# GpSimd's program of a graph-network stack written out per tile, with indices and records read in place

## The chip, the cores and the metric

The kernel runs on one core of one Trainium2 chip. The metric is the device time of one execution in microseconds. The engines are named as in the profile: PE is TensorE (matmul; PEld its weight loads), DVE is VectorE, ACT is ScalarE, POOL is GpSimd, SP is SyncE. A "q" behind a name (POOLq) is the engine's sequencer.

## The reference

Four graph layers run one after the other on 3125 nodes with 128 features and 50,000 weighted edges. Each layer normalizes the rows, applies relu, computes a message pass over the edges, and adds the result to x:

```
x = x + L0(relu(norm(x)))   # 2 weighted sums over edges, hop 1 and hop 2, gated
x = x + L1(relu(norm(x)))   # 4-head attention, softmax over a source's edges
x = x + L2(relu(norm(x)))   # 2 transformer convolutions (4 heads, then 2)
x = x + L3(relu(norm(x)))   # degree-normalized sum over edges
# the edge step of all: out = segment_sum(weight * v[one end], other end, n)
```

So everything is one pattern: fetch a node's row for each edge, weight it, and sum by the node at the other end.

## The kernel before, in words

**The sort.** The 3125 nodes are 25 blocks of 128 (NB). Edges are sorted into tiles of 128 edges so that all edges of a tile end in one block; there are T = 416 tiles, in two orders: by source (order 0) and by destination (order 1). VectorE computes for each edge, 400 per partition (J = 400), its row in the sorted list (rowI) and its record (recE: the other end's index, the place in the block, and for order 0 the weight). POOL scatters the records to DRAM with indirect DMAs of 128 edges each, 400 per order (`scatter`); SP brings them back as `rec[o]`, 128 partitions x 416 tiles.

**The sweeps.** Nine sweeps go over all 416 tiles, in 26 rounds (G) of U = 16 tiles, and each round in two halves of HU = 8. For each tile POOL issues one indirect DMA that fetches 128 rows of a node table into `ring`, a buffer of 16 tiles (two halves), taking its 128 indices from SBUF (`gathers`). The sweeps in order: L0h1 and L0h2 (weighted sums), L1A (maxima), then L1B, which gathers nothing, L1C, L2A (maxima), L2C, L2D, L2F, and L3 (sum). VectorE builds one-hot matrices from `rec`, TensorE multiplies them with the gathered rows and so sums by block in PSUM.

**What sets the order on POOL.** One instruction list: scatter of order 0; L0h1; L0h2; the first 8 of 25 rounds of the scatter of order 1; L1A; the remaining 17 rounds, beside L1B; L1C; L2A; L2C; L2D; L2F; L3. Before each half POOL waits for its credit, a semaphore that says the half's ring slots are free: `_product` (TensorE's last matmul of the half's previous use; L0h1, L0h2, L1C, L3) or `_used` (the others; line 522). The consumers wait for `s_gath`, which the gathers raise in groups of four tiles. In the scatter POOL waits for the landing of the DMAs that last used the half's staging slots (line 494).

The scatter copies 8 indices and 8 records into `sc_idx` and `sc_rec` (496, 497), waits (498), and issues 8 DMAs (501). `sem_inc(s_gate, 1)` after each wait is an instruction of the sequencer.

## Time and profile before

| | us |
|---|---|
| median of 3 runs | 8649.6 (8616.2 to 8651.0) |
| span of the profiled execution | 8657.7 |
| POOL busy | 4762.3 (55%) |
| PE busy | 4601.0 (53%) |
| DVE busy | 3781.0 (44%) |
| ACT busy | 1975.5 (23%) |

No time of the profiled execution is given apart from its span, which is 8 us over the median of the runs. Busy time is the sum of an engine's instructions, without register, branch, semaphore and DMA-issuing ones; POOL's indirect DMAs count as busy while GpSimd works on them. A share of the whole span averages over stages whose limits differ.

### The profile page before, as it was taken

What the parts mean: (1) busy time and instruction counts of PE and PEld (TensorE: products, weight loads), DVE (VectorE), ACT (ScalarE), POOL (GpSimd) and SP (SyncE); (2) the same over time, 40 slices, a digit from 0 to 9 for tenths busy, and PEclk for the clock granted to TensorE, in tenths of its full rate; (3) what the DMA queues carried; (4) which work ended last, traced back from release to release, by engine and by line L of the source; (5) the groups of instructions that cost most, each with busy time, mean ns of one, the idle gap of its engine ahead of it and who ended that gap; (6) DMA issues with size and microseconds to landing.
All of it is one profiled execution on the core that took longest, in us unless ns stands there. A gap on an engine that the chain in (4) does not pass through costs nothing.

```text
span 8657.7 us, 87742 instructions
## 1 busy us (share of the span) xinstructions
PE 4601.0 (53%) x14994; PEld 2464.6 (28%) x14995; DVE 3781.0 (44%) x7905; ACT 1975.5 (23%) x8567; POOL 4762.3 (55%) x5225
## 2 busy tenths in 40 slices
PE   0002443332455314555677767877889986673333
PEld 0001333332111113443322222333334433442333
DVE  7501221224466525333577776663146664456111
ACT  0000000000000001101455556774024433342000
POOL 1776666677666772774344435552035645552775
PEclk9997555555566555555899988887765555555555
DMA  1000112111100002222111112221023333332112
GB/s 26 4 1 23 44 44 34 23 23 9 12 1 1 17 17 55 70 69 43 36 44 41 42 30 56 54 55 41 16 72 92 96 72 91 89 94 43 46 45 40
DMA packets 246350, 370.54 MB, mean 43 GB/s; under 512 B 111935, under 2 KB 138020, under 8 KB 246308
## 3 DMA queue, kind: packets, MB, share of 16 engines
q0 software_dynamic: 158720, 263.93, 13.5%
q1 hardware_dynamic: 87588, 106.14, 4.3%
q8 instruction: 15, 0.25, 0.0%
q14 instruction: 27, 0.22, 0.0%
HBM read 351.69 MB, written 18.07 MB: 43 GB/s over the span
## 4 chain that ended last, share of the span: by engine, by line
PE 27%; POOL 20%; issue 20%; DVE 10%; another core or an unknown queue 6%; ACT 6%; DVEq 1%; DMA 1%; POOLq 0%; ACTq 0%; SPq 0%; PEld 0%; PEldq 0%
POOL work L529 18%; PE ps L1465 7%; PE ps L1567 7%; PE ps L1449 3%; PE ps L1447 3%; ACT work L1266 2%; ACT ps L1203 2%; PE ps L1389 2%; POOL rec_by_dst L501 1%; DVE acc L803 1%; PE ps L1610 1%; DVE work L739 1%; POOL idx_slot L524 1%; DVE work L1039 1%
## 5 line engine op out<-in xcount | busy, mean ns | idle before, releaser
L529 POOL DMA_INDIRECT work<-t_h,idx_slot x1248 | 1254.4, 1005 | 482.3 <-issue 384.4
L529 POOL DMA_INDIRECT work<-t_v,idx_slot x1248 | 1238.0, 992 | 476.8 <-issue 411.9
L1567 PE MATMUL ps<-work 128*128 128x512 f32 (+1 forms) x1664 | 977.1, 708 | 308.1 <-ACT work L1266 199.4
L1345 PE MATMUL ps<-work 128*128 128x128 f32 (+1 forms) x2496 | 703.0, 453 | 819.5 <-DMA work<-t_v,idx_slot 419.1
L524 POOL COPY idx_slot<-rec_d 128x8 int32 x312 | 71.7, 230 | 1770.5 <-DVEq L838 484.2
L1465 PE MATMUL ps<-big,work 128*128 x1664 | 988.1, 689 | 84.3 <-issue 27.3
L803 DVE TENSOR_REDUCE acc<-ps 128x512 f32 (+3 forms) x1248 | 743.6, 598 | 386.5 <-PE ps L1449 236.6
L1266 ACT ACTIVATE work<-work 128x128 f32<-128x128 f32 x2496 | 795.6, 390 | 297.6 <-PE ps L1567 179.8
L1203 ACT ACTIVATE ps<-ps 128x128 f32<-128x128 f32 x2496 | 662.0, 265 | 836.6 <-DVE ps L799 630.4
L1345 PEld LDWEIGHTS ps<-work 128*128 128x128 f32 x2496 | 593.4, 328 | 892.0 <-issue 870.6
L1447 PE MATMUL ps<-work 128*128 128x512 bf16 (+1 forms) x1248 | 579.5, 464 | 318.1 <-DVE acc L803 142.4
L1033 DVE TENSOR_TENSOR acc<-acc,ps 128x512 f32 (+1 forms) x832 | 461.1, 554 | 560.8 <-PE ps L1571 307.7
L799 DVE TENSOR_TENSOR ps<-ps,work 128x512 f32<-128x512 f32 (+1 forms) x832 | 465.7, 561 | 263.1 <-PE ps L1465 128.7
L1449 PE MATMUL ps<-work 96*128 96x512 bf16 (+1 forms) x1248 | 567.5, 455 | 0.0
L654 DVE TENSOR_TENSOR work<-rec_s,iota_f 128x1024 bf16<-128x1024 f32 x104 | 127.8, 1229 | 941.9 <-remote 389.9
L529 POOL DMA_INDIRECT work<-t_xl,idx_slot x416 | 451.5, 1085 | 157.4 <-issue 121.1
L1567 PEld LDWEIGHTS ps<-work 128*128 128x128 f32 x1664 | 355.0, 264 | 630.6 <-ACT work L1266 462.8
L529 POOL DMA_INDIRECT work<-t_k,idx_slot x416 | 423.9, 1019 | 159.9 <-issue 120.3
L501 POOL DMA_INDIRECT rec_by_src<-sc_rec_s,sc_idx x400 | 407.1, 1018 | 152.9 <-issue 117.2
L529 POOL DMA_INDIRECT work<-t_sj,idx_slot x416 | 401.5, 965 | 156.9 <-issue 133.8
L501 POOL DMA_INDIRECT rec_by_dst<-sc_rec_d,sc_idx x400 | 401.3, 1003 | 154.9 <-issue 138.2
L1203 ACT ACTIVATION_READ_ACCUMULATOR ps<-ps 128x1 f32 x2496 | 474.2, 190 | 46.8 <-issue 45.5
(315 smaller groups left out, 5883.9 us busy)
## 6 DMA issues: line engine op xcount, KB each, us to landing
work<-relT_by_dst SPq DMA_DIRECT2D x260, 256.0 KB
work<-t_v,idx_slot POOLq DMA_INDIRECT x1248
work<-t_h,idx_slot POOLq DMA_INDIRECT x1248
work<-relT_by_src SPq DMA_DIRECT2D x52, 256.0 KB
work<-t_sj,idx_slot POOLq DMA_INDIRECT x416
work<-t_xl,idx_slot POOLq DMA_INDIRECT x416
work<-t_k,idx_slot POOLq DMA_INDIRECT x416
rec_by_src<-sc_rec_s,sc_idx POOLq DMA_INDIRECT x400
```

The source lines that it names most:

```text
L501: nc.gpsimd.indirect_dma_start(rec_dram[o], bass.IndirectOffsetOnAxis(ap=sc_idx[:, k:k + 1], axis=0), sc_rec[o][:, k, :], None).then_inc(s ...
L529: nc.gpsimd.indirect_dma_start(col[:, k, 0:width], None, table, bass.IndirectOffsetOnAxis(ap=idx_slot[:, k:k + 1], axis=0)).then_inc(s_gat ...
L799: V.tensor_tensor(q, q, g, ALU.mult).then_inc(sig(nq, "_multiplied"), 1)
L803: V.tensor_reduce(tile_mx[:, ds(i * U + h * HU + k, 1), 0:H].rearrange("p a h -> p (a h)"), ps[:, 4 + k % 2, 0:H * P].rearrange("p (h e) - ...
L1033: V.tensor_tensor(part, part, ps[:, k % 4, 0:H * P].unsqueeze(1), ALU.add).then_inc(sig(name, "_added"), 1)
L1203: ins = A.activation(q, q, ACT.Copy, accum_out=aS[:, h * HU + k, hd:hd + 1])
L1266: ins = A.activation(wide[:, k % 2, hd * P:(hd + 1) * P], row, ACT.Copy, scale=pA[:, h, k % HU, hd:hd + 1])
L1345: ins = M.matmul(psum_blocks[:, ds(b, 1), 0:width], oh[:, k, :], ring[:, k, 0:width].unsqueeze(1), start=False, stop=False)
L1447: M.matmul(ps[:, 4 + k % 2, 0:w].rearrange("p (h e) -> p h e", h=H), ohm[:, h * HU + k, :], low_id.unsqueeze(1).to_broadcast([P, H, P]), s ...
L1449: M.matmul(ps[:, 4 + k % 2, 0:w], pick[0:R3, k, :], spread[0:R3, h, 0:w], start=False, stop=True)\
L1465: M.matmul(ps[:, k % 4, 0:w].unsqueeze(1), ohT[:, h, k * P:(k + 1) * P], table(blocks[k]), start=True, stop=True).then_inc(sig(nq, "_q"), 1)
L1567: M.matmul(ps[:, k % 4, 0:H * P], oh[:, k, :], wide[:, k % 2, 0:H * P], start=True, stop=True)\
```

## The change

The three staging buffers (`idx_slot`, `sc_idx`, `sc_rec`) and the semaphore `s_cp` go. POOL's loops over rounds are written out: one indirect DMA instruction for each tile, 400 + 400 in the scatters and 9 x 416 in the gathers. A gather's indices are column 0 of `rec[o]` at the tile, a scatter's are a column of `rowI[o]` and its data a record of `recE[o]`. The waits for credit stand where they stood, against constants. Other engines are not touched.

```diff
--- before.py
+++ after.py
@@ -140,7 +140,6 @@
         hT = carve(1920, [CN])
         vs = carve(2560, [CB, F])
         st = sb("st", [P, 64])
-        idx_slot = sb("idx_slot", [P, U], i32)
 
         ps = ctx.enter_context(nc.psum_tensor("ps", [P, 8, 512], f32))
         psf = ps[:, :, :].rearrange("p a b -> p (a b)")
@@ -175,8 +174,6 @@
         fill = [acc[:, 4 * o:4 * o + 4, :].rearrange("p a b -> p (a b)")[:, 0:TP * RW[o]] for o in (0, 1)]
         assert o1 + 448 + 2 * T <= NB * 512
 
-        sc_idx = sb("sc_idx", [P, U], i32)
-        sc_rec = [sb("sc_rec_s", [P, U, RW[0]]), sb("sc_rec_d", [P, U, RW[1]])]
         mapI = [bigf[:, o1 + 448 + o * T:o1 + 448 + (o + 1) * T].bitcast(i32) for o in (0, 1)]
         TQ = T // 4
 
@@ -241,7 +238,6 @@
         v_s = [sem("sort_dve_s"), sem("sort_dve_d")]
         s_pref = sem("prefix")
         s_pos = sem("rows_ready")
-        s_cp = sem("scatter_slots_filled")
         s_sc = [sem("scatter_half0"), sem("scatter_half1")]
         s_scd = sem("scatter_order_done")
         s_gate = sem("pool_gate")
@@ -486,26 +482,15 @@
                     pool.wait_ge(s_filled, 32)
                     pool.sem_inc(s_gate, 1)
 
-                def body(i, first):
-                    for h in (0, 1):
-                        j = i * U + h * HU
-                        if not first:
-
-                            pool.wait_ge(s_sc[h], (i + o * SG) * HU * 16)
-                            pool.sem_inc(s_gate, 1)
-                        nc.gpsimd.tensor_copy(sc_idx[:, h * HU:(h + 1) * HU], rowI[o][:, ds(j, HU)]).then_inc(s_cp, 1)
-                        nc.gpsimd.tensor_copy(sc_rec[o][:, h * HU:(h + 1) * HU, :], recE[o][:, ds(j, HU), :]).then_inc(s_cp, 1)
-                        pool.wait_ge(s_cp, (i + o * SG) * 4 + 2 * h + 2)
+                for j in range(start * U, end * U):
+                    h, turn = (j // HU) % 2, j // U + o * SG
+                    if j % HU == 0 and turn:
+
+                        pool.wait_ge(s_sc[h], turn * HU * 16)
                         pool.sem_inc(s_gate, 1)
-                        for k in range(h * HU, (h + 1) * HU):
-                            nc.gpsimd.indirect_dma_start(
-                                rec_dram[o], bass.IndirectOffsetOnAxis(ap=sc_idx[:, k:k + 1], axis=0),
-                                sc_rec[o][:, k, :], None).then_inc(s_sc[h], 16)
-
-                if start == 0:
-                    body(0, o == 0)
-                with pool.Fori(max(start, 1), end) as i:
-                    body(i, False)
+                    nc.gpsimd.indirect_dma_start(
+                        rec_dram[o], bass.IndirectOffsetOnAxis(ap=rowI[o][:, j:j + 1], axis=0),
+                        recE[o][:, j, :], None).then_inc(s_sc[h], 16)
                 if end == SG:
                     for h in (0, 1):
                         pool.wait_ge(s_sc[h], (o + 1) * SG * HU * 16)
@@ -517,18 +502,13 @@
                 used = sig(name, "_product" if name in SUMS else "_used")
                 if name not in SUMS:
                     credit(pool, name, "_used", 2)
-                with pool.Fori(0, G) as i:
-                    for h in (0, 1):
-                        pool.wait_ge(used, nth(name, i) * 2 + h + 1)
+                for t in range(T):
+                    if t % HU == 0:
+                        pool.wait_ge(used, nth(name, 0) * 2 + t // HU + 1)
                         pool.sem_inc(s_gate, 1)
-                        nc.gpsimd.tensor_copy(idx_slot[:, h * HU:(h + 1) * HU],
-                                              rec[o][:, ds(i * U + h * HU, HU), 0].bitcast(i32)).then_inc(ph("indices"), 1)
-                        pool.wait_ge(ph("indices"), (i + rounds[name] * G) * 2 + h + 1)
-                        pool.sem_inc(s_gate, 1)
-                        for k in range(h * HU, (h + 1) * HU):
-                            nc.gpsimd.indirect_dma_start(
-                                col[:, k, 0:width], None, table,
-                                bass.IndirectOffsetOnAxis(ap=idx_slot[:, k:k + 1], axis=0)).then_inc(s_gath[k // QU], 16)
+                    nc.gpsimd.indirect_dma_start(
+                        col[:, t % U, 0:width], None, table,
+                        bass.IndirectOffsetOnAxis(ap=rec[o][:, t, 0:1].bitcast(i32), axis=0)).then_inc(s_gath[t % U // QU], 16)
 
             scatter(0, 0, SG)
             pool.wait_ge(s_rec, 16)
```

What stands on POOL in the sweep L0h1, before. The loop runs 26 times; `idx_slot` are the staged indices, `t_v` is the table, `work` holds the ring:

```order
44 L524 ISA [waits L0h1_product]
45 L524 COPY idx_slot<-rec_s 128x8
46 L529 DMA work<-t_v,idx_slot 128x128 [waits indices]
47 L529 DMA work<-t_v,idx_slot 128x128 x7
48 L522 REGISTER_ALU
49 L524 ISA [waits L0h1_product]
50 L524 COPY idx_slot<-rec_s 128x8
51 L529 DMA work<-t_v,idx_slot 128x128 [waits indices]
52 L529 DMA work<-t_v,idx_slot 128x128 x7
53 L520 REGISTER_ALU
54 L520 COMPARE_AND_BRANCH
```

The same place now, the first three halves of 52:

```order
114 L509 DMA work<-t_v,rec_s 128x128 [waits scatter_half0,scatter_half1,rec_back,n0_table,L0h1_product]
115 L509 DMA work<-t_v,rec_s 128x128 x7
116 L509 DMA work<-t_v,rec_s 128x128 [waits L0h1_product]
117 L509 DMA work<-t_v,rec_s 128x128 x7
118 L509 DMA work<-t_v,rec_s 128x128 [waits L0h1_product]
119 L509 DMA work<-t_v,rec_s 128x128 x7
```

Eight DMAs follow eight with one wait between them, that for the credit; copy, wait for the copy, and branch are gone.

POOL's loop in the scatter of order 0, before, one of its two halves (`big` holds rowI and recE):

```order
26 L496 ISA [waits scatter_half0]
27 L496 COPY sc_idx<-big 128x8
28 L497 ISA
29 L497 COPY sc_rec_s<-big 128x24
30 L498 ISA
31 L501 DMA rec_by_src<-sc_rec_s,sc_idx 54528x3 [waits scatter_slots_filled]
32 L501 DMA rec_by_src<-sc_rec_s,sc_idx 54528x3 x7
```

and now, two halves:

```order
18 L491 DMA rec_by_src<-big 54528x3 [waits scatter_half0]
19 L491 DMA rec_by_src<-big 54528x3 x7
20 L491 DMA rec_by_src<-big 54528x3 [waits scatter_half1]
21 L491 DMA rec_by_src<-big 54528x3 x7
```

Both copies and the wait for them are gone; the wait for the DMAs of the half before last stays.

## Rows read from the trace of the kernel before

**Rows 1.** The page: busy time of the engines, and POOL in 40 slices.
```profile
PE 4601.0 (53%) x14994; PEld 2464.6 (28%) x14995; DVE 3781.0 (44%) x7905; ACT 1975.5 (23%) x8567; POOL 4762.3 (55%) x5225
...
POOL 1776666677666772774344435552035645552775
```

**Rows 2.** Windows: stretch, its length, busy us (instructions) by engine, clock, DMA share, GB/s.
```profile
180.00:757.00 577.00, 20.21 (x79) 16.62 (x79) 152.00 (x275) 13.20 (x19) 424.45 (x498) 1.00 0.03 4
769.00:1404.00 635.00, 301.90 (x1263) 244.77 (x1261) 126.56 (x105) 0.00 (x0) 432.40 (x468) 0.51 0.18 43
1419.00:2027.00 608.00, 201.67 (x822) 182.97 (x822) 121.97 (x100) 0.00 (x0) 428.63 (x471) 0.50 0.14 23
...
3398.00:4036.00 638.00, 340.21 (x1661) 284.23 (x1662) 202.66 (x416) 64.01 (x104) 463.56 (x468) 0.50 0.30 68
4194.00:5150.00 956.00, 711.43 (x2101) 260.21 (x2102) 697.49 (x1377) 562.91 (x3504) 418.65 (x467) 0.93 0.17 42
...
7993.00:8609.00 616.00, 220.18 (x846) 186.88 (x844) 63.06 (x52) 0.00 (x0) 428.24 (x468) 0.50 0.19 44
```

**Rows 3.** Timeline of POOL in L0h1: start, duration, operation, [idle before, releaser].
```profile
1020.27 0.95 POOL L529 DMA_INDIRECT work<-t_v,idx_slot  x1 [0.30 <-issue]
1021.23 0.19 POOL L524 COPY idx_slot<-rec_s 128x8 int32 x1
1022.23 0.98 POOL L529 DMA_INDIRECT work<-t_v,idx_slot  x1 [0.81 <-issue]
```

**Rows 4.** Timeline of POOL in the scatter of order 0, from its first copy.
```profile
413.01 0.20 POOL L496 COPY sc_idx<-big 128x8 int32 x1
...
414.15 0.98 POOL L501 DMA_INDIRECT rec_by_src<-sc_rec_s,sc_idx  x1 [0.81 <-POOL sc_rec_s L497]
```

**Rows 5.** Waits for gathered rows (L0h2, L3, L1C): total us, times, longest.
```profile
PE ps L1345 <- DMA work<-t_v,idx_slot: 414.6, 103, 15.5
...
PE ps L1345 <- DMA work<-t_h,idx_slot: 395.8, 104, 8.2
...
DVE zE L950 <- DMA work<-t_xl,idx_slot: 138.6, 50, 10.3
```

**Rows 6.** Waits of POOL's copy in L0h1, L0h2, L3 and L1C.
```profile
POOL idx_slot L524 <- remote: 32.5, 13, 2.9
...
POOL idx_slot L524 <- remote: 19.5, 8, 3.3
...
POOL idx_slot L524 <- remote: 17.0, 7, 3.2
...
POOL idx_slot L524 <- remote: 3.7, 2, 1.9
```

**Rows 7.** Waits of POOL's copy in L2A and L1A.
```profile
POOL idx_slot L524 <- DVEq L838: 365.0, 49, 9.3
...
POOL idx_slot L524 <- DVEq L818: 53.1, 11, 7.2
```

**Rows 8.** Timelines of SP and POOL where L1A's gathers begin.
```profile
2193.29 0.37 SPq L420 DMA_DIRECT2D t_sj<-node  x1
...
2209.48 0.20 POOL L524 COPY idx_slot<-rec_s 128x8 int32 x1
```

**Rows 9.** VectorE in two windows of L1B, and its waits in the first.
```profile
2911.00:3247.00 336.00, 92.78 (x278) 0.50 0.10 22
3255.00:3388.00 133.00, 89.03 (x283) 0.50 0.16 49
...
DVE work L754 <- remote: 186.9, 20, 29.5
```

**Rows 10.** The page: the DMA queues that carry instructions.
```profile
q8 instruction: 15, 0.25, 0.0%
q14 instruction: 27, 0.22, 0.0%
```

**Rows 11.** Timeline of POOL in L3, a pause without a releaser.
```profile
8008.74 1.99 POOL L529 DMA_INDIRECT work<-t_h,idx_slot  x1 [2.04 <-issue]
```

## The prediction

> **What bounds the kernel now.** I read the page first. GpSimd (POOL) is busy 55% of the span and has work in nearly every slice from 180 us to the end, a stretch of two slices in the third quarter aside [rows 1], yet a mean says little here, because the kernel is a row of sweeps with different limits. So the second view was the table of windows, one window a stage [rows 2]. In five of them POOL is busy 68 to 74% while TensorE is busy 4 to 53% and VectorE 10 to 32%: the scatter of the source records (180 to 757), L0h1 (769 to 1404), L0h2 (1419 to 2027), L1C (3398 to 4036) and L3 (7993 to 8609). In L2A TensorE and VectorE are each busy over 70%, POOL 44%.
>
> The third view is POOL's timeline. Inside a half (8 tiles) one indirect DMA takes 0.95 us and the next starts 0.30 us after it. Between two halves stands the copy of 8 indices: 0.19 us, and then 0.81 us until the first DMA of the new half [rows 3]. From the end of one half's last DMA to the next one's first it is 1.01 us instead of 0.30. In the scatter there are two copies, and it is 1.15 us instead of 0.30 [rows 4]. A half is thus 10.7 us of which 0.7 is the copy and the wait for it.
>
> Fourth, the lists of waits say whether that 0.7 us is on the path. In L0h2 TensorE waited 103 times, 414.6 us, for gathered rows, in L3 104 times, 395.8 us; in L1C VectorE waited for them 50 times, 138.6 us [rows 5]. Those sweeps go at POOL's pace. The other way round, POOL's copy was held up by its credit (the release of a ring half) 13 times in L0h1, 8 in L0h2, 7 in L3, twice in L1C [rows 6], but 49 times in L2A, 365 us, and 11 times in L1A [rows 7]. In L2A, L2C, L2D, L2F and mostly in L1A POOL waits for the others, so a faster POOL buys nothing in the steady part.
>
> **The change part by part.** It takes away every copy on POOL and the wait behind it, 468 halves of gathers and 100 of scatters, and the loop instructions. The DMAs, their sizes, the credits and the ring with its two halves stay; the other four engines keep their programs. Per half I expect the gap to become 0.30 us, that of two DMAs in a row: saved 0.70 us in a gather and 0.85 us in a scatter. A wait with a semaphore increment stands in that gap still. What it costs behind a DMA no row shows; the nearest rows are 0.30 us (nothing between) and 0.81 us (a wait for a copy just done) [rows 3]. I take 0.30, since the copy itself starts 0.01 us after the DMA before it although the same credit wait stands ahead of it: a wait that is already satisfied is run through while the DMA is at work.
>
> The sum, against this execution's span of 8657.7 us:
> - First scatter: 49 gaps x 0.85 = 42 us. TensorE is busy 20 us and VectorE 152 of 577 there [rows 2], and the records must be back before L0h1, so all of it counts.
> - L0h1: 51 gaps less the 13 where the credit came late [rows 6], since what POOL gained in the half before is waited away there: 38 x 0.70 = 27 us. In a blocked half the way from credit to first DMA gets shorter too (no copy); bounds 0 and 1.19 + 0.81 us each. I take 3 us for all, 30.
> - L0h2: 43 x 0.70 = 30 us. L3: 44 x 0.70 = 31 us.
> - L1C: 49 x 0.70 = 34 us. Late credit is rare, so the limit behind POOL has room.
> - First third of the destination scatter, 16 halves before L1A: POOL would be done 13 us earlier, but the table that L1A's gathers read is sent only at 2193.29, some 16 us before POOL is free at 2209.48 [rows 8], and has to land. 7 us.
> - The rest of that scatter, 34 halves, runs beside L1B and is shorter by 34 x 0.85 = 29 us. L1B does not need it, yet while it runs L1B crawls: VectorE does 278 instructions in 336 us, afterwards 283 in 133 us [rows 9], and its waits there, 186.9 us in 20 times, name no releaser. If the crawl goes by time, an end 29 us earlier gives 29 x (1 - 0.83/2.13) = 18 us; if it goes by the number of scatter DMAs, about 3. I take 12.
> - Starts of L1A and of the four L2 sweeps: about 1 us each, 5 us.
> Together 42 + 30 + 30 + 31 + 34 + 7 + 12 + 5 = 191 us: a span of 8467. The median of the runs shown, 8649.6, lies 8 us under the profiled span, so 8459, 2.2% less.
>
> What is late next: in the POOL-bound sweeps still POOL, by 0.94 + 0.30 us a tile, 10.0 us a half. The ring has two halves and the consumer answers one half later, so a half that is 0.7 us shorter also leaves it 0.7 us less. The 28 late credits of L0h1, L0h2 and L3 may become more; they are blank waits ("remote"), so I can't tell their cause.
>
> **The price of a straight program.** Before, POOL runs loops of some 16 DMAs; after, each of the 4544 indirect DMAs is an instruction of its own that has to be brought in. The profile shows instruction traffic of 15 + 27 packets, 0.47 MB, for all engines together [rows 10]. Pauses of POOL with no releaser are there too, 2.04 us, with a longer DMA behind [rows 11]; they come in the loops as well, about every 110 DMAs, so they aren't the price of a straight program and stay. A DMA takes 1.25 us with its gap, so a block of instructions lasts POOL a long time, and I take 0; the bounds are 0 and a pause of 2.04 us per block, of unknown number.
>
> The Trainium skill has a rule on it (Runtime: NRT & Kernel Launch, Instruction fetch mechanics): the sequencer brings in the next 16 KiB, 256 instructions, while it executes, and only a taken branch out of its window stalls it. By that rule fetching costs nothing, and the sum above stands. Should every such block cost a pause all the same, by the page's size it would be some 10 pauses in those stages, about 20 us. No row here shows a straight POOL program, so the rule is untried by this trace.
>
> **Rivals.**
> 1. Fetching is seen, mildly: one pause of 2.04 us every 128 DMAs. The five POOL-bound stages and the destination scatter hold 2464 DMAs (400 + 4 x 416 + 400), so 19 x 2.04 = 39 us: 8498. For it: pauses of that size exist. Against: in the loops they come without any new code. Chance 0.12.
> 2. The gap isn't the copy's. The 0.81 us belongs to a wait instruction ahead of a DMA, and the credit wait inherits it. Then only the copies go, 0.20 us a gather half and 0.34 a scatter half: 49 x 0.34 + 174 x 0.20 and some us for the rest = about 60 us: 8590. For it: 0.81 follows a wait every time. Against: the copy's immediate start, above. Chance 0.07.
> 3. The late credits take it. In the sums sweeps the consumer's signal comes at its own time, POOL only waits longer, and the destination scatter's end gives nothing. First scatter aside nothing is left, and the crawl beside L1B, with denser DMAs, is 15% worse (50 us): 8650 - 42 + 50 = 8658. For it: blank waits of 3 us in three sweeps and up to 29.5 us in L1B. Against: 38 to 49 of 51 halves show no late credit. Chance 0.06.
> 4. The other way: the blank waits belong to POOL's loop and copies and go with them. L1B's 336 us at the fast rate would be 131, and the 28 blocked halves lose 69 us of waiting [rows 6]: about 250 us on top, 8210. Nothing but coincidence in time speaks for it. Chance 0.05.
> 5. Slower: POOL starves for instructions. Place: the same 2464 DMAs. Each pause costs 2.04 us, so the gain of 191 us is eaten at 94 pauses, one every 26 DMAs; at one every 16 it is 154 x 2.04 = 314 us, and the time is 8459 + 314 = 8773. For it: POOL's program held 224 indirect DMAs, which loops ran again and again, and holds 4544 now. Against: 0.47 MB of instructions in the whole span cost no visible stall of POOL. Chance 0.07.
>
> **How the numbers follow.** My forecast has 0.63, with a range of its own from 8410 to 8515: its ends are the gap at 0.45 instead of 0.30 with 3 us for L1B, and blocked halves that gain their full 2 us with 18 us for L1B. The predicted time is 8459. For eight times in ten I go from 8395 to 8595, which takes in rivals 1 and 2. A difference of 0.5%, 43 us, is about what a measurement of this kernel can tell from none: faster 0.63 + 0.12 + 0.07 + 0.05 = 0.87, within it 0.06 (rival 3), slower 0.07.
>
> **What would show it.** In the changed profile POOL has no copies, and the gap between two indirect DMAs across a half's edge reads 0.30; reading 0.8 there is rival 2. The first scatter lasts about 535 us instead of 577, L0h1 605, L0h2 578, L1C 604 and L3 585. L2A to L2F keep their lengths within 2 or 3 us each; were they shorter by 30 us, my reading of who waits there would be wrong. Instruction packets grow; pauses beyond those every 110 DMAs would be rivals 1 or 5. In L1B the number and length of the waits without a name tell between my 12 us and rivals 3 and 4.

## The result: 3.4% slower

The changed kernel takes 8915.4 us (median of 4 runs, 8908.4 to 8948.2), the kernel before beside it 8636.8 (8616.2 to 8651.0): ratio 1.034, interval 1.030 to 1.038. I had forecast 8459. The profiled execution's span is 8906.4 us, 248.7 more than before.

The page of the changed kernel, the rows that answer to [rows 1] and [rows 10]:

```profile
PE 4622.6 (52%) x14994; PEld 2467.6 (28%) x14995; DVE 3792.7 (43%) x7905; ACT 1979.3 (22%) x8567; POOL 4568.4 (51%) x4557
...
POOL 1775666775466760666144434444015554552675
...
q14 instruction: 63, 0.52, 0.0%
```

POOL has 668 instructions fewer (5225 before) and 194 us less busy time. The busy time of the others hardly moved: what was added is waiting. In POOL's slices the 10th has gone from 7 to 5, the 11th from 6 to 4 and the 16th from 2 to 0.

Windows of the changed kernel (stretch, length, busy us and instructions of PE, PEld, DVE, ACT, POOL, then clock, DMA share, GB/s), which answer to [rows 2]:

```profile
180.00:714.00 534.00, 20.21 (x79) 16.61 (x79) 121.60 (x225) 13.20 (x19) 405.84 (x400) 1.00 0.03 4
781.00:1388.00 607.00, 299.24 (x1230) 239.48 (x1228) 126.07 (x104) 0.00 (x0) 422.86 (x416) 1.00 0.18 45
...
3585.00:4206.00 621.00, 333.46 (x1630) 278.15 (x1630) 200.49 (x411) 63.78 (x103) 427.52 (x416) 0.50 0.31 70
...
8252.00:8843.00 591.00, 214.65 (x826) 182.85 (x825) 64.02 (x54) 0.00 (x0) 422.60 (x414) 0.50 0.19 46
```

The first scatter got its 42 us. But VectorE did 225 instructions in that window; before it did 275 there. The sweep L0h1 starts at 780.6, 66.2 us after POOL had finished. TensorE's granted clock in L0h1 reads 1.00 (2.4 GHz) here and 0.51 (1.2 GHz) before. It explains nothing: TensorE is busy 299 and 302 us there, and a repetition of the changed kernel (e7 below) takes the same 607 us at 0.50.

POOL's timeline in L0h1, across the edge of a half, answers to [rows 3]:

```profile
1048.70 0.94 POOL L509 DMA_INDIRECT work<-t_v,rec_s  x1 [0.30 <-issue]
1049.95 0.94 POOL L509 DMA_INDIRECT work<-t_v,rec_s  x1 [0.30 <-issue]
1051.20 0.94 POOL L509 DMA_INDIRECT work<-t_v,rec_s  x1 [0.30 <-issue]
```

Copies and rests are gone, and the median gap over an edge is 0.30 to 0.31 us in both scatters, L0h1, L0h2 and L3, as forecast. So POOL does what the change says, and the time is lost elsewhere. Stage by stage, from POOL's first indirect DMA of a stage to its last (or to the first of the next sweep, where the wait between counts):

| stage | before | after | difference | forecast |
|---|---|---|---|---|
| first scatter to start of L0h1 | 590.6 | 600.6 | +10 | -42 |
| L0h1 | 622.0 | 607.1 | -15 | -30 |
| L0h2 | 605.9 | 593.0 | -13 | -30 |
| first third of the second scatter to start of L1A | 183.5 | 292.6 | +109 | -7 |
| L1A | 646.7 | 655.1 | +8 | -1 |
| rest of the second scatter (beside L1B) to start of L1C | 540.4 | 629.4 | +89 | -12 |
| L1C | 624.0 | 621.3 | -3 | -34 |
| L2A | 945.0 | 943.7 | -1 | -1 |
| L2C | 742.8 | 819.5 | +77 | -1 |
| L2D and L2F together | 1450.9 | 1449.3 | -2 | -2 |
| L3 | 603.9 | 590.8 | -13 | -31 |

Three rows hold most of the loss, and the first row lost a gain of 42 us. In three of these four VectorE should work beside POOL's scatter; the fourth is L2C. VectorE's windows of the changed kernel, first beside the scatter, then with POOL waiting, twice over:

```profile
2007.00:2172.00 165.00, 34.57 (x95) 0.50 0.06 2
2172.00:2300.00 128.00, 54.36 (x128) 0.51 0.07 5
2956.00:3311.00 355.00, 55.69 (x145) 0.52 0.04 6
3311.00:3585.00 274.00, 164.97 (x520) 0.50 0.15 44
```

and of the kernel before, the whole first third of its second scatter:

```profile
2027.00:2210.00 183.00, 89.58 (x223) 0.50 0.14 12
```

The 223 instructions that fitted into 183 us are now 95 beside the scatter and 128 behind it. In L1B it is 145 in 355 us (2.4 us each) and then 520 in 274 (0.5 us each); in [rows 9] it was 278 in 336 us and 283 in 133. SP and POOL where L1A begins answer to [rows 8]: the table goes out at 2290.86 instead of 2193.29, and POOL has stood idle for 128.71 us.

```profile
2290.86 0.37 SPq L416 DMA_DIRECT2D t_sj<-node  x1
```
```profile
2300.35 0.97 POOL L509 DMA_INDIRECT work<-t_sj,rec_s  x1 [128.71 <-POOLq L286]
```

What VectorE does there in detail. Its timeline in the changed kernel beside the scatter:

```profile
2056.23 0.17 DVE L697 TENSOR_TENSOR st<-acc,st 128x5 f32<-128x5 f32 x1 [1.19 <-issue]
2057.64 0.17 DVE L698 TENSOR_SCALAR st<-st 128x5 f32<-128x5 f32 x1 [1.24 <-issue]
2059.03 0.17 DVE L699 TENSOR_TENSOR st<-st 128x5 f32<-128x5 f32 x1 [1.22 <-issue]
2061.13 0.19 DVE L700 RECIPROCAL st<-st 128x5 f32<-128x5 f32 x1 [1.93 <-issue]
2062.53 0.17 DVE L701 TENSOR_TENSOR st<-st 128x5 f32<-128x5 f32 x1 [1.21 <-issue]
```

Each instruction takes its usual 0.17 us, but the next one starts 1.4 to 2.1 us later, and no engine is waited for ("issue"). The page doesn't count register instructions; the trace has them, and they take more than half of that time, while nothing is recorded in the rest (start, duration, operation of VectorE's sequencer):

```
2056.88 0.71 FUSED_REGOPS
2058.28 0.70 FUSED_REGOPS
2059.69 1.39 ALU_OP
2061.77 0.70 ALU_OP
```

The median of such an instruction on VectorE is 0.04 us (ALU_OP) and 0.065 us (FUSED_REGOPS). I count the instructions of the sequencer that work on registers, branch or load a value and take over 0.5 us, and call them slow register instructions: VectorE 556 after and 47 before, TensorE 242 and 97, SP 110 and 74. On VectorE 302 lie between the start of the first scatter and L0h1, 99 between that of the second and L1A, 65 in its rest. VectorE's waits in the changed kernel's L1B answer to the wait in [rows 9]:

```profile
DVE work L734 <- remote: 145.8, 4, 41.0
```

Four waits of 36 us in the mean, and none has a releaser. In the one that ends at 3137.2 (24.8 us) TensorE runs eight matmuls of 0.17 to 0.19 us, with register instructions of 0.7 to 1.4 us between them: what VectorE waits for there is another slow sequencer. Signals are late as well. In L1C, POOL's sequencer passes the credit some 2.5 us (median) after TensorE's last matmul of the half has ended, wherever POOL is blocked. In L0h1, VectorE starts over 2 us (up to 8.7) after the matmul that it waits for in 19 of 40 waits; in the kernel before it was so in 15 of 40 (up to 8.9).

So beside a stream of indirect DMAs without rests the sequencers of other engines run slowly, and that is what the experiments look at.

### The profile page after: what moved, and what is told of

Its sections match the earlier page's. It is cut to its first block, busy times and chain, and to the rows that moved or that the text cites. A ratio compares the mean times of both kernels' runs of the same rounds, so it can differ in the third digit from the quotient of the medians.

```text
span 8906.4 us, 84294 instructions
## 1 busy us (share of the span) xinstructions
PE 4622.6 (52%) x14994; PEld 2467.6 (28%) x14995; DVE 3792.7 (43%) x7905; ACT 1979.3 (22%) x8567; POOL 4568.4 (51%) x4557
## 4 chain that ended last, share of the span: by engine, by line
PE 28%; issue 18%; POOL 18%; DVE 10%; ACT 7%; another core or an unknown queue 6%; DVEq 4%; DMA 2%; ACTq 0%; SPq 0%; POOLq 0%; PEldq 0%
POOL work L509 18%; PE ps L1547 7%; PE ps L1445 6%; PE ps L1429 4%; ACT ps L1183 3%; PE ps L1427 3%; ACT work L1246 2%; PE ps L1369 2%; DVE acc L783 1%; PE ps L1590 1%; DVEq L20 1%; DVE work L719 1%; PE ps L1325 1%; ACT work L1172 1%
## 5 line engine op out<-in xcount | busy, mean ns | idle before, releaser
L509 POOL DMA_INDIRECT work<-t_h,rec_d x1248 | 1241.4, 995 | 1482.9 <-DVEq L818 418.4
L1547 PE MATMUL ps<-work 128*128 128x512 f32 (+1 forms) x1664 | 1003.1, 727 | 325.4 <-ACT work L1246 212.6
L509 POOL DMA_INDIRECT work<-t_v,rec_s x832 | 844.6, 1015 | 448.5 <-issue 245.7
L509 POOL DMA_INDIRECT work<-t_k,rec_d x416 | 413.1, 993 | 728.6 <-DMA t_v<-big 408.3
L509 POOL DMA_INDIRECT work<-t_xl,rec_d x416 | 427.9, 1029 | 467.2 <-DMA t_xl<-node 273.8
L509 POOL DMA_INDIRECT work<-t_sj,rec_s x416 | 414.5, 996 | 369.3 <-issue 129.9
L509 POOL DMA_INDIRECT work<-t_v,rec_d x416 | 424.6, 1021 | 348.4 <-DVEq L1014 159.4
L491 POOL DMA_INDIRECT rec_by_src<-big x400 | 406.2, 1015 | 305.2 <-issue 305.2
L491 POOL DMA_INDIRECT rec_by_dst<-big x400 | 394.0, 985 | 126.1 <-issue 126.1
```

What stands on the lines that cost most here:

```text
L491: nc.gpsimd.indirect_dma_start(rec_dram[o], bass.IndirectOffsetOnAxis(ap=rowI[o][:, j:j + 1], axis=0), recE[o][:, j, :], None).then_inc(s_ ...
L509: nc.gpsimd.indirect_dma_start(col[:, t % U, 0:width], None, table, bass.IndirectOffsetOnAxis(ap=rec[o][:, t, 0:1].bitcast(i32), axis=0)). ...
L1547: M.matmul(ps[:, k % 4, 0:H * P], oh[:, k, :], wide[:, k % 2, 0:H * P], start=True, stop=True)\
```

## The experiments

**How to read them.** The kernel before read two very different times: 8637, 8813 and 8644 us in three comparisons, and 8049, 8060, 8055 and 8048 us in four others. I call the surroundings of the first three H (high) and of the other four L (low). The first experiments (L) and the next two (H) ran on the same chip some minutes apart, so it is neither the kernel nor the chip. Under L every profile has 15 slow register instructions on VectorE, 4 on TensorE and none on SP, in whichever kernel; all 19 are loads of a value, and no other one is above 0.5 us. No profile of the kernel before was taken under L; e1, which takes the same time there (1.001), stands in for it.

The traces carry a second mark. Each L trace holds 94,769 to 96,126 records of a semaphore's update, each H trace 33,854 to 47,002. For the first scatter there are 6,960 in e1 and 6,804 in e15 (both L); under H there are 6,246 in the kernel before and 853 in the changed kernel. So records are missed where the sequencers are slow. A wait without a releaser ("remote") can mean only that the record of its release is missing: VectorE has 180 such waits in the kernel before and 213 in the changed one, and no engine has one in any L trace. All times here come from recorded executions, so whether the recording itself has a part in H was not tested.

I compare only kernels that were measured together, beside the same kernel before. Theory A: POOL's rests at the edges of a half let the other sequencers work. Theory B (and B'): the written-out program does the harm, by its fetching. Theory C: the surroundings decide. Theory E: reading in place does it, whatever the rest.

**First experiments, L (before 8049.1 us).** e1: the loops written out, copies kept.

```diff
-                if start == 0:
-                    body(0, o == 0)
-                with pool.Fori(max(start, 1), end) as i:
-                    body(i, False)
+                for i in range(start, end):
+                    body(i, o == 0 and i == 0)
...
-                with pool.Fori(0, G) as i:
+                for i in range(G):
```

> The kernel before with its copies, slots and waits for them, only its POOL loops written out per round (4544 DMA instructions, as in the changed kernel). Theory A, the pause: what slows VectorE, TensorE and SyncE is that POOL no longer rests about 1 us per half; here it does, so 8600 to 8680 us, no more than 60 slow register instructions (0.7 us) of VectorE in the whole run, L1A's gathers start near 2210 us. Theory B, the straight program: its fetching or its constant waits do it, so 8850 us or more, and L1A starts near 2300.

e2: the changed kernel with a rest at each edge of a half, a memset of 8 columns and a wait for it.

```diff
+                nc.gpsimd.memset(pause[:, :], 0.0).then_inc(s_pause, 1)
+                paused[0] += 1
+                pool.wait_ge(s_pause, paused[0])
+                pool.sem_inc(s_gate, 1)
...
+                    if j % 8 == 0:
+                        rest_a_while()
...
+                    if t % 8 == 0:
+                        rest_a_while()
```

> The changed kernel (indices and records read in place, straight program) with one idle step ahead of each half: POOL zeroes 8 columns of a scratch tile and waits for that. Theory A, the pause: the gap at a half's edge is back to about 1.0 us and the time to 8600 to 8690 us, the first scatter about 570 us, L1A near 2210. Theory B, the straight program or the reading in place: still 8850 us or more, and the gap is only added on top.

e3 has only the changed kernel's `scatter` in the kernel before, e4 only its `gathers`; the other function is as it was.

> Scatters as in the changed kernel (in place, straight, no pause), gathers as before (copies, loops). Theory A, the pause: the harm sits where a scatter runs beside VectorE's own work, so most of the loss is here: the stretch from L0h2's last gather to L1A's first about 290 us instead of 185, L1A's last to L1C's first about 630 instead of 542, L1 up; 8780 to 8900 us. If the gathers did the harm, about 8600 us.

> Gathers as in the changed kernel, scatters as before (copies, loops). Theory A, the pause: 15 + 13 + 13 + 3 us come out of the sums sweeps and L1C, and L2C may lose up to 77 us as in the changed kernel: 8600 to 8700 us. If the gathers did the harm, 8850 or more.

Measured: e1 8061.3 us, 1.001 (1.000 to 1.002); e2 7950.4, 0.987 (0.986 to 0.989); e3 7972.3, 0.990 (0.989 to 0.992); e4 7882.9, 0.980 (0.978 to 0.981). Each part is a gain here and the written-out program costs nothing. That contradicts the first comparison so plainly that I ran the changed kernel again.

**Second experiments, H (before 8812.6 us).** e5 is the changed kernel, e6 the kernel before, both as they are.

> The changed kernel unchanged, once more, beside the kernel before. In the first four experiments the kernel before took 8049 us instead of 8637, and none of the 0.7 us register instructions showed. Theory C, the surroundings: where those slow instructions are absent the change does what was forecast, ratio 0.965 to 0.98 (7760 to 7890 us against 8049), with L1A's gathers starting 135 us or less after L0h2's last one. If they are present, the ratio is near 1.03 again. Theory D, both parts together: scatters and gathers in place each gained alone (0.990, 0.980), but together POOL never rests and the ratio is above 1 also where the kernel before takes 8049.

> The kernel before, unchanged, with a trace that stands beside that of the repeated changed kernel. Theory C: with 8049 us it has L1B at about 5.2 us a half also beside the scatter, and no run of 0.7 us register instructions on TensorE, VectorE or SyncE; with about 8640 us it has them as the first trace.

e5: 9048.2 us, 1.030 (1.023 to 1.036), 531 slow register instructions on VectorE. e6: 8853.8 us in one run, 157 of them, 102 in the first third of the second scatter; its L1A starts 93.9 us late where the first profile of before had 1 us. So the kernel before is slowed under H too, only less, and in that place its rests did not prevent it.

**Third experiments, H (before 8643.7 us, 19 runs).** e7 is the changed kernel, e8 is e2 again, e9 is e1, e10 is e4.

> The changed kernel as it is. Two cases, told apart by the kernel before in the same comparison. If that reads near 8050 us and its trace shows few register instructions above 0.5 us (under 20 on VectorE), both theories say that the two parts add up: 0.990 x 0.980 = 0.970, near 7810 us, with L1B hidden beside the destination scatter. If it reads near 8800 us with about 50 to 160 such instructions on VectorE, then VectorE shows over 400 of them here, the gap before L1C is 270 to 290 us, and the ratio is 1.03, as in the two comparisons of this kind so far.

> The changed kernel with one small memset of 8 columns and a wait for it at each edge of a half, so that GpSimd rests about 1 us after 8 indirect DMAs as it did before; indices are still read in place. Theory A (the rest at the edge is what lets the other engines' sequencers read their instructions in time): where the before kernel is near 8800 us, this one is not slower than it, ratio 0.985 to 1.00, VectorE's register instructions above 0.5 us are under 200 and the gap before L1C is 110 to 160 us. Theory B (it is not the rest but reading indices at an offset in the large array, or the written-out program): ratio 1.02 to 1.03 with over 400 slow register instructions, like the changed kernel. Where the before kernel is near 8050 us: 0.987 again, and it tells nothing between the theories.

> The kernel before with GpSimd's loops written out tile by tile, its index copies kept. Theory A: 1.00 within 0.01 in either condition, since the rests are still there. Theory B' (the written-out program, whose instructions have to be brought in all the time, slows the fetching of the other engines): where the before kernel is near 8800 us, ratio 1.02 to 1.03 with over 400 slow register instructions on VectorE and a gap before L1C of 250 us or more.

> Only the gathers read their indices in place; the scatters keep both copies and rests. Where the before kernel is near 8050 us: 0.980 again. Where it is near 8800 us: Theory A puts the harm beside L1B on the scatter, which is as before here: the gap before L1C is 110 to 160 us instead of 285, L0h1 to L1C are 13 us shorter each, and L2C keeps its 50 to 75 us of harm; ratio 0.995 to 1.005. Theory B' (written-out program): the gap before L1C is above 250 us all the same, ratio 1.02 or more.

| us | e7 changed | e8 rests | e9 written out | e10 gathers in place |
|---|---|---|---|---|
| ratio (interval) | 1.030 (1.025-1.036) | 1.020 (1.014-1.026) | 0.995 (0.992-0.998) | 1.011 (1.006-1.016) |
| median | 8908.6 | 8811.4 | 8612.0 | 8707.4 |
| wait of POOL before L0h1 | 66.8 | 12.7 | 12.8 | 12.5 |
| wait before L1A | 138.5 | 30.8 | 9.8 | 12.5 |
| L1A | 652.3 | 643.0 | 638.2 | 654.9 |
| scatter beside L1B + wait before L1C | 640.6 | 619.9 | 491.7 | 539.3 |
| L2C | 803.2 | 784.1 | 768.4 | 821.4 |
| VectorE, slow register instructions | 549 | 76 | 54 | 87 |
| TensorE, slow register instructions | 226 | 182 | 108 | 206 |

The rows below the median come from one profile each. That of e8 was its fastest run, 8743.1 us, 68 under its median, so its column shows less than it lost.

e9 ends theory B as a cause by itself: the program is as long as the changed one (73 instruction packets against 63) and it is the fastest of the four. Whether writing out does harm only where the rests are missing, no run under H says: none takes the rests away and keeps the loops. The Trainium skill (Runtime: NRT & Kernel Launch, Instruction fetch mechanics) says that a sequencer fetches ahead while it executes and stalls only on far branches; e1 (1.001) and e9 (0.995) agree with it.

e10 keeps the copies in the scatters and loses no time before L0h1 or L1A, so those two losses, 54 and 126 us, belong to the scatter in place. So do 101 us around L1B. The gathers in place lose in L1A (17 us), in L2C (53) and in L2D (20: 731.3 against 711.0). Around L1B, e10 (539.3) takes what the kernel before took (540.4) and e9 48 us less; the scatters of the first two are loops and that of e9 is written out.

e8 against e7 differs only in the rests. By the medians they bring back 97 of the 265 us that e7 loses against the kernel before; e8 is still 2.0% slower. The wait before L0h1 goes entirely, and the one before L1A mostly. VectorE in e7, one round of a loop beside the scatter (POOL's last DMA ends at 713.0), and two rounds after it:

```profile
607.18 0.49 DVE L598 TENSOR_SCALAR big<-big 128x400 f32<-128x400 f32 x1 [6.36 <-issue]
607.87 0.57 DVE L599 TENSOR_TENSOR big<-big 128x400 f32<-128x400 f32 x1 [0.20 <-DVE big L598]
610.67 0.65 DVE L600 SCALAR_TENSOR_TENSOR big<-big 128x416 f32<-128x416 f32 x1 [2.23 <-issue]
617.67 0.49 DVE L598 TENSOR_SCALAR big<-big 128x400 f32<-128x400 f32 x1 [6.35 <-issue]
...
740.64 0.49 DVE L598 TENSOR_SCALAR big<-big 128x400 f32<-128x400 f32 x1 [0.53 <-DVE big L600]
741.16 0.58 DVE L599 TENSOR_TENSOR big<-big 128x400 f32<-128x400 f32 x1
741.89 0.65 DVE L600 SCALAR_TENSOR_TENSOR big<-big 128x416 f32<-128x416 f32 x1 [0.15 <-DVE big L599]
743.07 0.49 DVE L598 TENSOR_SCALAR big<-big 128x400 f32<-128x400 f32 x1 [0.53 <-DVE big L600]
```

and the same loop in e8, where the scatter runs on until 748.1:

```profile
318.13 0.49 DVE L612 TENSOR_SCALAR big<-big 128x400 f32<-128x400 f32 x1 [0.36 <-DVE big L609]
318.65 0.58 DVE L613 TENSOR_TENSOR big<-big 128x400 f32<-128x400 f32 x1
319.39 0.65 DVE L614 SCALAR_TENSOR_TENSOR big<-big 128x416 f32<-128x416 f32 x1 [0.16 <-DVE big L613]
320.58 0.49 DVE L612 TENSOR_SCALAR big<-big 128x400 f32<-128x400 f32 x1 [0.54 <-DVE big L614]
```

A round takes 10.5 us beside the scatter without rests (most of the others there 11.2), 2.43 once it is over, and 2.45 beside the scatter with a rest of 0.9 us per 8 DMAs. The other profiles under H agree: mostly 11.2 us in the first one of the changed kernel and in e5, and 2.4 to 2.6 in the first one of the kernel before, e9 and e10. The work is the same and its parts of `big` don't overlap with POOL's; in e7 and e8 only the rest differs. Under H this is the cleanest pair I have, and it shows theory A beside the first scatter. Before L1A the wait fell from 138.5 to 30.8 us in this pair, yet it was 93.9 in e6 with all copies and rests, so there the rest helps and is not enough. On TensorE the rests take away little (226 to 182 slow register instructions; 108 in e9, which has rests and copies).

Around L1B it fails by half. I expected 110 to 160 us before L1C and measured 241. VectorE beside the scatter, e8 and then e10:

```profile
2850.00:3229.00 379.00, 67.29 (x181) 0.51 0.04 8
```
```profile
2850.00:3240.00 390.00, 130.71 (x373) 0.51 0.08 19
```

and e9, whose scatter is written out as that of e8 is:

```profile
2850.00:3245.00 395.00, 164.55 (x475) 0.52 0.11 25
```

The scatters have nearly the same rests, 0.91 us in e8 and 1.12 in the other two, but e8 gets 181 instructions of VectorE through, e10 373 and e9 475. Whether the missing 0.2 us decide or the reading in place itself (theory E) is not told apart by these. In its profile e8 takes 128 us more than e9 around here, which is all that it takes more in the whole span (129).

The loss in a sweep has another form. POOL in L1C of e10:

```profile
3505.39 0.94 POOL L523 DMA_INDIRECT work<-t_xl,rec_d  x1 [0.30 <-issue]
3509.22 1.43 POOL L523 DMA_INDIRECT work<-t_xl,rec_d  x1 [2.89 <-remote]
3510.96 0.94 POOL L523 DMA_INDIRECT work<-t_xl,rec_d  x1 [0.30 <-issue]
```

Every second half begins with a credit that POOL waits 2.9 us for. L1C takes 621.8 us here, and 623.0 in e9 with the 34 us of copies.

**Fourth experiments, L (before 8060.2 us).** e11 is the changed kernel with `rest_a_while()` at `j % 4 == 0` in the scatters alone. e12 is e1 with one more rest in the middle of each half beside L1B:

```diff
+                            if start and k % HU == HU // 2:
+                                rest_a_while()
```

e13 is e3 again. e14 is e1 with `gathers` in place for four sweeps:

```diff
+                if name in ("L0h1", "L0h2", "L1C", "L3"):
+                    for t in range(T):
...
+                            bass.IndirectOffsetOnAxis(ap=rec[o][:, t, 0:1].bitcast(i32), axis=0)).then_inc(s_gath[t % U // QU], 16)
+                    return
```

> The changed kernel with a rest (small memset and a wait for it, 0.6 us more between two DMAs) every 4 DMAs of both scatters; the gathers stay in place without rests. If the amount of rest sets how far VectorE, TensorE and SyncE are slowed beside the scatter (theory A), and the kernel before reads above 8600: first scatter about 600 us, no slow register instructions of VectorE in it, L1A starts under 40 us after the first third, and the destination scatter's rest plus the gap before L1C is 500 to 560 us (changed kernel 640, before 538), ratio 1.00 to 1.01, L2C still 820. If reading in place does it whatever the rest (theory E): scatter plus gap stays above 600 and the ratio above 1.02. Where the kernel before reads near 8050: scatters longer by 60 us in all, 0.985 to 0.99.

> The kernel before with loops written out, its copies kept, and one more rest in the middle of each half of the destination scatter's part beside L1B (34 rests, about 21 us longer). Theory A, where the kernel before reads above 8600: L1B gets on faster beside it, so scatter plus gap before L1C falls from 492 to 538 us to 430 to 480; ratio 0.985 to 0.99. Theory E or one in which L1B is slowed by the number of DMAs alone: scatter plus gap the same or 20 us longer, ratio 0.995 to 1.00. Where the kernel before reads near 8050, L1B is hidden and it is 20 us longer, 1.003.

> Only the scatters in place; the gathers keep copies and rests. Where the kernel before reads above 8600: the part carries the loss around L0h1 (start late by 50 us, first scatter shorter by 42), before L1A (110 to 130 us gap) and before L1C (gap 270 to 290 instead of 150), so 1.02 to 1.025, while L1A, L2C and L2D keep the lengths of before (640, 743 to 771, 710 us). If the losses before L1A and L1C come from the gathers' side instead: under 1.01. Where it reads near 8050: 0.990 again.

> Loops written out; copies kept in the scatters, L1A, L2A, L2C, L2D and L2F; indices read in place in L0h1, L0h2, L1C and L3, where GpSimd sets the pace. Where the kernel before reads above 8600: theory A says the harm of the gathers in place is in L1A, L2C and L2D, which are as before here, so what is left is 11 + 7 + 0 to 30 + 10 us of gain: ratio 0.985 to 0.995, L2C 745 to 770 us and the gap before L1C 97 to 150. If an earlier dense sweep slows the later ones: L2C above 800 all the same. Where it reads near 8050: 16 + 13 + 50 + 20 = about 100 us less, 0.988.

Measured: e11 7937.2 us, 0.985 (0.984 to 0.987); e12 8099.0, 1.005 (1.004 to 1.007); e13 7979.6, 0.990 (0.988 to 0.992); e14 7967.0, 0.989 (0.987 to 0.990). All are near what was written for L; e12 is 39 us longer where 20 were expected. Under L rests only cost time. What they do under H, which their other numbers are about, stays unmeasured.

**Fifth experiment, L (before 8055.3 us).** e15 is the changed kernel.

> The changed kernel as it is, to see it beside its own kernel before once more. Where that reads near 8050 us (few slow register instructions): theory A and C together say 0.970, near 7820 us, no gap over 15 us before L1A and L1C, fewer than 20 slow register instructions of VectorE. Where it reads 8600 to 8810: 1.03 as three times before. A theory in which the change itself brings the slow instructions in, whatever the surroundings: 1.03 in both.

7803.3 us (7783.9 to 7807.1), ratio 0.968 (0.966 to 0.970). The very kernel that loses 3% three times under H gains 3.2% here. Its POOL streams just as densely: median gap 0.30 us over the edges of the scatter beside VectorE's work and of L1B. The same lines of VectorE as above, in e15:

```profile
1952.90 0.17 DVE L697 TENSOR_TENSOR st<-acc,st 128x5 f32<-128x5 f32 x1
1953.10 0.17 DVE L698 TENSOR_SCALAR st<-st 128x5 f32<-128x5 f32 x1
1953.30 0.17 DVE L699 TENSOR_TENSOR st<-st 128x5 f32<-128x5 f32 x1
1953.50 0.19 DVE L700 RECIPROCAL st<-st 128x5 f32<-128x5 f32 x1
```

Four starts within 0.6 us instead of 4.9, beside the same stream. e15 has 15 slow register instructions on VectorE. Its windows for VectorE, beside the first third of the second scatter and beside the rest of it:

```profile
1881.00:2051.00 170.00, 89.61 (x223) 0.51 0.08 2
2609.00:2969.00 360.00, 223.62 (x663) 0.51 0.16 37
```

All 223 instructions and nearly all of L1B fit beside the scatters, and POOL waits 3.9 us before L1A and 10.7 before L1C. In L0h1, VectorE starts 0.17 us after the matmul that it waits for, all 50 times. Theory C holds: the stream without rests does no harm by itself; it does where the surroundings are H.

**Sixth experiments, L (before 8048.2 us).** e16, e17 and e18 are e12, e13 and e14 once more.

> Written-out loops, copies kept, one more rest in the middle of each half of the scatter part beside L1B. Where the kernel before reads above 8600, theory A (rests set how far L1B is slowed): scatter plus gap before L1C 430 to 480 us instead of 492 to 538, ratio 0.985 to 0.99. If the slowing goes by the number of DMAs: 510 to 540, ratio 0.995 to 1.00. Near 8055: 1.005 as measured.

> Only the scatters in place. Where the kernel before reads above 8600: L0h1 starts as late as before although the scatter ends 42 us earlier, gap before L1A 110 to 130 us, before L1C 270 to 290, L1A, L2C, L2D as before; 1.02 to 1.025. If the gathers' side causes the gaps: under 1.01. Near 8055: 0.990 as measured twice.

> In place only in L0h1, L0h2, L1C and L3. Where the kernel before reads above 8600: 0.985 to 0.995, L2C 745 to 770 us and the gap before L1C 97 to 150 us, if the harm of the gathers lies in L1A, L2C and L2D; L2C above 800 if an earlier dense sweep does it. Near 8055: 0.989 as measured.

Measured: e16 8098.8 us, 1.006 (1.004 to 1.008); e17 7974.9, 0.991 (0.989 to 0.993); e18 7973.2, 0.991 (0.989 to 0.992). They repeat e12, e13 and e14 within 0.2% and decide nothing about H.

No version beats both kernels in both surroundings. Under L it is the changed kernel itself, 0.968. Under H it is e9 by 0.5%, which is as small as the difference that I had called measurable. e14 keeps the copies wherever a loss was seen under H; that it would be the safe choice is an inference, since it ran only under L.

## Why the prediction was wrong

**The step that failed** is "the other four engines keep their programs", with the work that was to hide each edit. I asked of each rest only whether it lies on POOL's own path, and costed it for the others at nothing, or at a gain (L1B, 12 us). Under H VectorE's sequencer keeps its pace beside the first scatter only where POOL rests (e7 against e8), and work that was hidden comes to lie on the path. The rests are not all of it: with them back and the reading still in place (e8), 168 of the 265 us lost are lost still. Between my sum (-191) and the two spans (+249) lie 440 us. By the table 52 of them came before L0h1, 116 before L1A, 101 before L1C and 78 in L2C, together 347; of the other 93, 81 are gains that came too small in L0h1, L0h2, L1C and L3, 9 are L1A, and 3 lie outside the table.

**First scatter, -42.** Right for POOL (-42), wrong for the path. I wrote that VectorE is busy 152 of 577 us, so all of it counts. A quarter busy is true at VectorE's usual pace. With 1.4 us from one short instruction to the next, its work outlasts the scatter. e7 against e8 shows it.

**L0h1, L0h2, L3, -30 each.** 13 to 15 came under H, 13 to 24 under L (e1 to e15, which were not measured together: 572.9 to 556.4, 576.0 to 563.4, 579.1 to 555.6; e4, measured with e1, gives 16, 13 and 20). The edge gap is 0.30, as I took it, so rival 2 is refuted. But the DMAs themselves became longer: 1.033 us in the mean in L0h1 of e15, 0.972 in e1, which over 416 is 25 of the 36 us that 52 edges save. The term was right in kind and too large by half.

**L1C, -34.** -3 under H and -48 under L. Under H the late credit [rows 6] takes it, which I had judged rare because it stood at 2 of 51: with 0.7 us less slack it came 24 times in the changed kernel (68.2 us) and in e10 (67.8 us). Under L it came in none, and the DMAs there were shorter too (1.060 us against 1.092), which is 13 us of the 48. The prediction had named this as what could be late next, and gave it no price.

**First third of the second scatter, -7.** I read from [rows 8] that POOL was free 16 us after the table was sent, and took the table's time as fixed. It was set by VectorE beside the same scatter, and moved by 97.6 us. Under H it was not even fixed in the kernel before (e6).

**L1B, -12.** I saw the crawl [rows 9], and that it has blank waits up to 29.5 us, and asked only how long it would last. That its depth could change was in rival 3, as 15%. It went from 1.2 to 2.4 us for each instruction of VectorE (336/278 in the window of before, 355/145 in that of after).

**The sweeps that don't wait for POOL.** I said that L2A to L2F keep their lengths within 2 or 3 us. L2C gained 77. POOL's waits for its credit there, in the changed kernel, and ACT's waits with it:

```profile
POOL work L509 <- DVEq L1014: 294.8, 50, 10.9
...
ACT pE L1232 <- issue: 98.8, 35, 7.1
```

Before, the same two were 138.2 us in 49 and 23.2 us in 9. In these 98.8 us ScalarE waits for nothing that the profile shows. That the copies in the gathers go is enough for it (e10, 821.4 against 768.4 in e9). The size is rough: L2C reads 819.5, 816.9 and 803.2 in the three profiles of the changed kernel and 742.8 and 770.8 in the two of the kernel before. Why L2C and not L2A, the runs don't say.

**The rivals.** Rivals 1 and 5, POOL starving for instructions, are refuted by e1 and e9, and by the changed trace: 63 packets instead of 27 and fewer pauses of 2 us than in the kernel before (25 and 41 inside the halves). Rival 5 had the right side for the wrong reason. Rival 4, blank waits that vanish with the copies, is refuted: under H POOL's went from 30 waits and 72.7 us to 45 and 141.3, and under L there are none with the copies either (e1). They belonged to H. Rival 3 was nearest in kind, but I had priced a deeper crawl at 50 us and its case at no change. The case that happened, a resource off the path whose rests the path needs, was not among them, and 0.07 for slower was too little when 186.9 of VectorE's 243 idle us in that window of L1B were already without a name.

**The forecast under L.** There, 252 us were gained (8055.3 to 7803.3) where I had 191. The sum missed L1A (-40; all four here are e15 against e1), L2C (-19) and L2F (-26), where I saw POOL waiting under H, and L1B (-38 instead of -12). So the size was too small there, the direction right. The profile that I read was one of H: its slow register instructions and its waits without a releaser were there to be found.

**What stays open.** What H and L are: the traces mark them (slow register instructions, missing update records), but no run here sets or removes either, and whether the recording has a part in it is not known. So the sign of the change, +3% or -3%, can't be foretold for a new occasion. Whether the rest must be over some length beside L1B or reading in place does harm of its own (e8 against e9 and e10). And by what way the stream slows other sequencers: the runs show that it does, not how.

## What to carry to other kernels

When an engine's pauses are taken away, ask who works in them, also on engines with no shared buffer: look beside that stream for "idle <-issue" between short instructions and for waits without a releaser, before the change. Such waits stood in the profile of before here, and stand in none of L. A wait behind a slow engine's work is not a fixed time. And where the same kernel reads two times that differ by 7 to 10%, repeat the comparison on another occasion before believing either sign; here it was 1.03 and 0.97.

## What was not expected of the hardware

- The same kernel read 8049 us and, some minutes later on the same chip, 8813. The difference sits in the sequencers: data instructions keep their durations (0.17 and 0.49 us in both), register instructions go from 0.04 to 0.70 us, and signals come late (in L1C 2.5 us after TensorE's last matmul). The Trainium skill (Perfetto Trace Analysis, Per-engine timelines) says that of a sequencer-only instruction the profiler reports the execution alone, and neither the wait nor the time its signal takes. In these traces the execution itself is longer, so the slowing can be counted.
- The two surroundings differ in what the trace itself holds: under H at most half of the semaphore updates are recorded that are recorded under L, and in the first scatter of the changed kernel one in eight (853 against 6,804). Waits without a releaser came under H alone.
- Under H a rest of 0.9 us per 8 indirect DMAs, 8% of POOL's time, was enough to bring VectorE's round beside the first scatter from 10.5 to 2.45 us. Beside L1B it was not (181 instructions in 379 us, 475 in 395 in e9).
- The mean duration of an indirect DMA moves when rests go, one way or the other by sweep. Under L (e4 against e1) it rose in L0h1 (0.972 to 1.034 us), L0h2 (0.980 to 1.049) and L3 (0.985 to 1.040) and fell in L1A (1.025 to 0.986), L1C (1.092 to 1.057), L2C (1.041 to 0.978) and L2D (1.052 to 0.971). In the first three, part of a rest that is removed comes back in the DMAs.
- Written-out code of 4544 indirect DMAs, with copies and rests kept, cost nothing (0.995 under H, 1.001 under L).
